# A graph kernel's node unit: its product moved from the end of its own slot behind the next slot's first dense pieces

## What is computed

```python
x = x + L0(relu(layernorm(x)))     # twice: sum over edges of (x @ W0 + b0)[src], beside x @ W1 + b1,
                                   #        joined by W2, then divided by the row's deviation
x = x + L1(relu(layernorm(x)))     # sum over edges of x[src] @ W + b, divided by the degree
x = x + L2(relu(layernorm(x)))     # three times: sum of (x @ W)[src] * dinv[src] * dinv[dst], + b, relu
x = x + L3(relu(layernorm(x)))     # an edge network on [h[src], h[dst]], summed by destination, and two node layers
```

## Time and profile before

| | us |
|---|---|
| three runs, median (lowest to highest) | 9854.04 (9832.5 to 9878.18) |
| the profiled execution | 9863.67 |
| its span (first to last instruction) | 9861.5 |
| PE busy, matmuls | 7828.0 (79%) |
| POOL busy | 5612.6 (57%) |
| DVE busy | 3557.3 (36%) |
| ACT busy | 1548.2 (16%) |
| mean granted share of TensorE's full clock | 0.888 |

### The profile page before, as it was taken

One profiled execution on the slowest core, in us unless ns is written; L12 is line 12 of the kernel. 1 busy time (PEld: TensorE's weight loads), 2 busy tenths in 40 slices (PEclk: granted clock), 3 DMA queues, 4 the chain that ended last, 5 costly groups with the idle time before them and its releaser, 6 DMA issues. The chain is left out here.

```text
span 9861.5 us, 153058 instructions
## 1 busy us (share of the span) xinstructions
PE 7828.0 (79%) x53210; PEld 5930.2 (60%) x53210; DVE 3557.3 (36%) x7241; ACT 1548.2 (16%) x3109; POOL 5612.6 (57%) x5798
## 2 busy tenths in 40 slices
PE   2888887888878888788887888788886777777777
PEld 1666665666656666566665665566665666666666
DVE  6777774233322222222221222222222333333333
ACT  3666663000000000000000000000000111111111
POOL 2555554555546656455546555455554666666665
PEclk9999998999979989888988989888987888888888
DMA  5232224444445555444454444445543444444443
GB/s 101 92 102 94 99 94 127 135 141 139 139 147 142 146 144 147 146 137 136 135 154 126 136 138 135 150 137 143 143 139 111 121 123 123 121 123 123 121 125 108
DMA packets 756941, 1268.18 MB, mean 129 GB/s; under 512 B 286468, under 2 KB 584647, under 8 KB 749591
## 3 DMA queue, kind: packets, MB, share of 16 engines
q1 hardware_dynamic: 476340, 779.09, 25.4%
q0 software_dynamic: 185344, 371.98, 16.0%
q10 hardware_dynamic: 94948, 113.19, 3.3%
HBM read 1076.55 MB, written 194.22 MB: 129 GB/s over the span
## 5 line engine op out<-in xcount | busy, mean ns | idle before, releaser
L2274 PE MATMUL PS<-PARTS,work 128*128 128x288 bf16 x26950 | 3854.7, 301 | 452.8 <-issue 415.2
L2274 PEld LDWEIGHTS PS<-PARTS,work 128*128 128x128 fp8e4 x26950 | 2759.3, 103 | 1368.5 <-issue 600.4
L724 POOL DMA_INDIRECT GF<-table,SRC x2262 | 2261.6, 1000 | 1576.3 <-issue 613.9
L735 POOL DMA_INDIRECT GF<-newparts,SRC x1760 | 1675.8, 952 | 1465.7 <-PE PS L2256 587.7
L735 POOL DMA_INDIRECT work<-newparts,SRC x1735 | 1646.2, 949 | 1089.1 <-PE PS L2256 532.7
L2220 PE MATMUL PS<-work 128*96 128x128 f32 x3126 | 595.4, 370 | 514.1 <-issue 283.9
L2388 PE MATMUL PS<-PARTS,work 128*128 128x289 bf16 x5390 | 981.1, 293 | 0.0
L1059 ACT ACTIVATE work<-PS 128x396 fp8e4<-128x396 f32 x1760 | 825.2, 502 | 553.5 <-PE PS L2325 441.9
L2220 PEld LDWEIGHTS PS<-work 128*96 128x96 f32 x3126 | 544.4, 236 | 545.6 <-issue 545.3
L2325 PE MATMUL PS<-FREE 128*128 128x396 bf16 x1760 | 600.1, 343 | 240.2 <-ACT work L1059 100.6
L1701 DVE TENSOR_TENSOR work<-PS,REL 128x1024 bf16<-128x1024 f32 (+1 forms) x636 | 771.4, 1214 | 0.4 <-issue 0.4
(11 more groups left out here) (276 smaller groups left out, 5987.9 us busy)
## 6 DMA issues: line engine op xcount, KB each, us to landing
work<-amat SPq DMA_DIRECT2D x1925, 224.0 KB
work<-in_dst_dram SPq DMA_DIRECT2D x195, 512.0 KB
amat<-work SPq DMA_DIRECT2D x55, 1568.0 KB
work<-in_edge_attr_dram SPq DMA_DIRECT2D x195, 384.0 KB
GF<-table,SRC POOLq DMA_INDIRECT x2262
PARTS<-newparts SPq DMA_DIRECT2D x35, 1008.0 KB, 10.2
GF<-newparts,SRC POOLq DMA_INDIRECT x1760
work<-newparts,SRC POOLq DMA_INDIRECT x1735
```

Source lines behind the costliest of these rows:

```text
L724: pool.indirect_dma_start(G[:, k, i, 0:D], None, table_rows[a % 2], bass.IndirectOffsetOnAxis(ap=SRC[:, tile:tile + 1], axis=0)).then_inc( ...
L735: pool.indirect_dma_start(GP[g % PLACE][:, i, :], None, part_rows[a % 2], bass.IndirectOffsetOnAxis(ap=SRC[:, tile:tile + 1], axis=0)).the ...
L2274: last = pe.matmul(PS[:, DENSE_B[b], 0:PQ], AB[m][:, jj * WIN:(jj + 1) * WIN].bitcast(FP8), PARTS[:, j * PQ:j * PQ + PQ], start=(j == 0), ...
```

## The change

In the turns the product of step 0 is no longer issued at the end of its half's own slot. It is issued in the next slot, behind a dense piece and the window's transpose: behind the second piece in `l0b`, `l1`, `l2a` and `l2b`, behind the first in `l2c`. Both halves move. In the slot's closing loop step 0 is left out for PE; the steps 1 to 3 stay. Neither ACT, DVE, POOL nor SP has another order, and `last_units` is as it was. The lines of the changed file stand two to four higher than here (2122 is 2124, 2274 is 2276).

```diff
+PRODUCT_AFTER = {"l0b": 1, "l1": 1, "l2a": 1, "l2b": 1, "l2c": 0}
...
                                 if s:
                                     turn_window(i, s - 1)
                                 else:
                                     turn_window(i - 1, SLOTS - 1)
+                            if q == SHARE[s][0] + PRODUCT_AFTER[PHASES[a + 1]] and not start:
+                                for half in range(HALVES):
+                                    if s == SLOT_OF[half] + 1:
+                                        step(S, a + 1, 0, True, half, i - 1)
                         gathered(i, s, last_turn)
                         for half in range(HALVES):
                             q = s - SLOT_OF[half]
-                            if start or not 0 <= q < 4:
+                            if start or not 1 <= q < 4:
                                 continue
                             step(S, a + 1, q, True, half, i - 1)
```

## The result

| | before | changed kernel |
|---|---|---|
| median of 20 runs each | 9862.52 us | 9837.99 us |
| lowest to highest | 9832.08 to 9893.63 | 9783.73 to 9855.89 |
| ratio, 95% interval | | 0.9967 (0.9957 to 0.9977) |
| profiled execution: span | 9861.5 us | 9781.6 us |
| mean granted share of TensorE's full clock | 0.888 | 0.898 |

The change gains 0.33% by the ratio, some 32 us (23 to 42); the two medians differ by 25 us. The forecast's sum had 60. The profiled execution of the changed kernel is the fastest of its 20, 54 us under their median, and 31 us of its lead are there ahead of the first moved product (ACT's first copy for a product in `l0b`'s turns stands at 1760.8 instead of 1791.8 us), so its trace shows more than the change is worth.

The account below looks back on a forecast made before the run. PE was taken as bound by waits for ACT's copy, a slot floor of 11.9 us and five-piece slots. Gains of 45 + 12 + 3 = 60 us gave a forecast of 9795 us, range 9735 to 9855.

Parts of the forecast that it names:

- What bounds the kernel: PE idles 154.1 us for ACT's copy ahead of products; four-piece slots sit at a floor, five-piece slots are PE-bound.
- The floor: In slots 3, 4 and 6, of four pieces: no slot goes below 11.9 us, cause unknown.
- Half 0 in l1, l2a, l2b, 45 us: Slot 1 falls from 13.60 to 12.1 us, 1.5 us per turn over thirty turns: 45 us gained.
- other slots, which the forecast had counted as 0: Slot 2, coming behind a slot at the floor, was counted 0, with +20 to -40 us for the range.
- Half 1, 0: No wait ahead of its product, dense products can use the stop instead: 0; otherwise a cost of 0.5 to 1 us per turn.
- second rival: Half 1's product was free in slot 4's stop and costs 1 to 1.9 us in slot 5: 9909 us, chance 0.08.
- its own sign of error: The forecast is wrong in its main step if slot 1 falls to the floor but another slot takes it up.
- Half 0 in l0b, 3 us: Waits there are small, so slot 1 gains at most 0.3 us per turn: 3 us.
- l2c, 12 us: Half 0 in l2c loses its 1.40 us wait less a few tenths, 1.2 us over ten turns: 12 us, ends 0 and 15.
- slot 1 also ends earlier: In l2c, h comes at 6582.0 instead of 6583.85 and slot 1 ends earlier, so the transposes' wait stays about the same.
- The clock, 0: PE's granted clock falls by the stop alone, also behind slot 4 without a wait for ACT, so nothing was counted.
- Rival 1: Slot 1 gets a stop of its own and stays at 13 us or so: 9844 us, chance 0.26.

Follow-up runs that it names:

- after2: The changed kernel timed again, against the kernel before in the group of 9866 us: 9844.92 us, ratio 0.9987.
- g6_before: The kernel before with six gathers and window products per window instead of eight in the five later aggregations: 8928.72 us, ratio 0.8839 to the kernel before.
- best2: Against the kernel before, only half 0's products of l1, l2a, l2b and l2c moved, in the group of 9866 us: 9815.56 us, ratio 0.9951.
- again: The changed kernel once more, in the group where the kernel before took 10104 us: ratio 0.9994 to the kernel before.
- before_copy: The kernel before once more, unchanged, in the group without the stop of PE: 8028 us.
- before2: The kernel before once more, unchanged, in a group with the stop of PE: 9866 us.
- gated2: best2 with POOL waiting, ahead of each window's fifth gather, for the rows of the first four: 9638.88 us, ratio 0.9776 to the kernel before.
- gated: The same kernel as gated2, timed in the group without the stop: 8744.04 us, ratio 1.0890 to the kernel before.

## Why the prediction was right or wrong

The sign and the range held, and the range proves little: it reached to 9855, 1 us above the 9854 from which it was counted, so any small gain would have fallen into it. The sum, 60 us, was nearly twice the 32 us of the first comparison and more than four times `after2`'s 13. What failed is a term: half 1's products were put at nothing.

*What bounds the kernel.* Right. The floor is POOL's group (`g6_before`: 9.2 us instead of 12), and the waits for ACT were not worth their 154 us.

*Half 0 in l1, l2a, l2b, 45 us.* Right in mechanism and about right in size: slot 1 fell to 12.15 to 12.34 instead of 12.1, 1.1 to 1.3 us per turn, 36 to 38 us. Most of what is missing is that 13.60, one turn's slot 1, stood for a mean of 13.45. By whole turns `best2` gained 51 us in these phases; the rest is in other slots, which the forecast had counted as 0, and in the scatter between traces.

*Half 1, 0.* This is the step that failed. I wrote that after the move as many dense products could go through the stop, and gave 0.5 to 1 us per turn only as an end. Timed, half 1 and `l0b` together cost 35 us (`best2` against `after2`). In slot 5, which PE bounds, the move costs 0.4 to 1.0 us per turn by the table, 23 us for the four phases, and less in the other pairs of traces. It is the second rival's mechanism at half of its price or less, and I had let it decide the sign only, instead of taking it as a term. The prediction named its own sign of error, that slot 1 falls but another slot takes it up. In `after2`'s `l1` this is what happened: slot 1 lost 1.3 us, slot 5 gained 1.0, and the turn stayed at 101.1.

*Half 0 in l0b, 3 us.* No trace shows a gain: both halves moved, the turn was the same in the first comparison (106.0) and grew by 0.7 us in the second (106.45 to 107.11); it has hardly a wait to lose. With six gathers its slot 1 grew by 0.3. Single traces can't fix so small a number.

*l2c, 12 us.* Too large by `best2`, which moves just these products there. Slot 1 fell by 0.64 us and the wait for h went, but slot 2 took it back (13.38 to 14.65 us), 0.1 us per turn in all; `after2`, with half 1 moved too, gained 0.9 (slot 2 at 13.80). The smaller step that failed: "slot 1 also ends earlier" was counted as if slot 2 would keep its length.

By the turns' column, ten turns each: `after2` +7 (`l0b`) - 0 - 5 - 5 - 9 = -12 us, measured -13 (-29 to +2). `best2` -4 - 15 - 16 - 20 - 1 = -56, measured -48 (-64 to -34).

*The clock, 0.* Half right. It did rise (0.888 to 0.898), and the product runs at 290 instead of 390 ns. Where slots sit at the floor nothing of it shows: slots 3, 4 and 6 stay at 11.9 to 12.0 us in `l2a` and `l2b`. Whether the higher clock gives `after2` its lead in `l2c` over `best2` is open. The rule of the Trainium skill (TensorE: Matmul & The Clock Gate, HAM oscillation) agrees with the rows of PE itself, where the product takes 2.45 us behind the wait of 4.16 us and 1.25 us at its new place; it speaks of PE's pace, and here PE's pace isn't the slot's. In `l2c` without the stop, where PE sets the pace, the wait and the clock together made PE's rows 4.8 us shorter, and half of it reached the turn.

*Rival 1* said that slot 1 gets a stop of its own. It did, as the rows after show, but the slot still came near the floor.

What I could not have read from one trace: that the floor is there in some groups of runs only. And a trace taken from the fastest of 20 runs showed a gain of some 50 us in the turns where the medians differ by 25 us.

## What to carry to other kernels

Price a moved instruction by two questions: what bounds the slot it leaves, and what bounds the slot it enters. Here half 0's product left a slot at POOL's floor for one that PE bounded only because of it, and gained; half 1's had no wait to lose and entered a slot of five pieces that PE bounds, and together with `l0b`'s it gave back 35 of 48 us: move only what waits. And before a stall is tuned around, ask whether it can be broken up: one wait in POOL's groups was worth another 1.8% on top of the better move in the group that has the stall, and cost 9% in one that hasn't.

## What the runs showed of the hardware

The kernel before took 8028, 9862 and 10104 us in different groups of runs; traces from them have granted clocks of 0.960, 0.888 and (of `again`) 0.886. Whether this goes with the chip, the machine or the time is not shown. The groups of 9862 us and more have a stop of PE that comes late in each group of eight indirect DMAs of POOL: "issue" ahead of pieces is 21 us in the group of 8028 us, 415 to 611 in the others. From first to last group of gathers the five phases take 4387 us in `before_copy` and 5556 in `before2`, 1169 of the 1827 us between their spans; the rest lies outside these phases and wasn't looked into. While the stop lasts PE gets through one to three products per 0.7 or 1.4 us, and its signals to the other engines are late as well: in the changed kernel DVE started 1.6 us behind the product's end. With six gathers in a group the "issue" time is 267 us. POOL's wait for the rows in `gated2` lasted 1.9 us from the end of a gather in the median, and as long in `gated`, without the stop; 98 of 100 waits were under 4.2 us. Behind eight gathers in a row it was 1.86 us, so their rows hadn't piled up there. What is short during the stop no run shows.
